# Shifted-window attention on one core: attention outputs computed feature-major in four column groups, softmax weights normalised before their transposition

## What is computed

```python
qkv = xw @ qkvw + qkvb                       # 512 windows of 7x7 = 49 tokens, 160 features
q, k, v = heads(q), heads(k), heads(v)       # 5 heads of 32 features
attn = softmax(einsum('whid,whjd->whij', q, k) * 32 ** -0.5 + bias + mask)
out = einsum('whij,whjd->whid', attn, v)     # back to 49 x 160
out = out @ projw + projb
x = x + out; x = x + gelu(ln(x) @ w1 + b1) @ w2 + b2
```

## Time and profile before

| | us |
|---|---|
| median of three runs | 3516.08 |
| profiled execution, its own time | 3515.67 |
| its span, first to last instruction | 3513.9 |
| TensorE matmuls busy | 3297.9 |
| VectorE busy | 2393.0 |
| ScalarE busy | 1878.0 |
| GpSimd busy | 833.1 |

### The profile page before, as it was taken

The page is one execution under the profiler, slowest core; times in us unless marked ns, Lnnn a source line. Parts: engine busy times, 40 slices in busy tenths (PEclk is TensorE's granted clock), DMA queues, the critical chain, the costliest instruction groups (busy, mean ns, idle before and its releaser), DMA issues. The chain is left out here.

```text
span 3513.9 us, 95515 instructions
## 1 busy us (share of the span) xinstructions
PE 3297.9 (94%) x35820; PEld 2960.7 (84%) x35820; DVE 2393.0 (68%) x6968; ACT 1878.0 (53%) x4454; POOL 833.1 (24%) x1625
## 2 busy tenths in 40 slices
PE   7995999999999999999999999999999999999679
PEld 6884888888888888888888888888888888888579
DVE  1114777777777777777777777777777777777322
ACT  1112555555555555555556666666666666666221
POOL 5300222222222222222222222222222222222110
PEclk9997999999999999999999999999999999999789
DMA  5321111111111111111111111111111111111275
GB/s 108 87 73 47 30 35 34 34 34 34 34 33 30 34 34 34 34 34 44 43 31 32 35 35 29 35 23 35 35 35 29 35 23 35 35 35 24 47 137 92
DMA packets 246486, 148.37 MB, mean 42 GB/s; under 512 B 31429, under 2 KB 245880, under 8 KB 246398
## 3 DMA queue, kind: packets, MB, share of 16 engines
q1 hardware_dynamic: 244694, 147.01, 18.7%
q0 software_dynamic: 1728, 0.48, 0.1%
HBM read 96.80 MB, written 52.50 MB: 42 GB/s over the span
## 5 line engine op out<-in xcount | busy, mean ns | idle before, releaser
L1350 PE MATMUL rm<-w,ht 128*112 128x160 f32 x4480 | 693.7, 304 | 0.0
L1350 PEld LDWEIGHTS rm<-w,ht 128*112 128x112 f32 x4480 | 608.8, 177 | 28.6 <-ACT ht L951 13.0
L951 ACT ACTIVATE ht<-rm 128x448 f32<-128x448 f32 (+1 forms) x640 | 319.2, 499 | 263.5 <-PE rm L111 258.1
L865 POOL TENSOR_TENSOR rs<-ln_tmp,mhalf 112x4 f32<-112x4 f32 (+1 forms) x128 | 125.6, 981 | 996.0 <-DVE ln_tmp L1031 996.0
L933 ACT ACTIVATE ot_hi<-ra 128x98 fp32r<-128x98 f32 x512 | 103.1, 257 | 455.0 <-PE ra L1329 455.0
L896 ACT ACTIVATE qm<-ra,qmask 128x392 f32<-128x392 f32 x512 | 259.0, 589 | 12.1 <-PE ra L111 3.2
L1298 PEld LDWEIGHTS s_ps<-kt,qm 128*49 128x49 f32 x8192 | 210.2, 126 | 48.9 <-issue 40.4
L111 PE MATMUL rm<-z2t_hi,w_hi 128*128 128x448 f32 (+1 forms) x640 | 248.1, 388 | 1.3 <-DVE z2t_rest L1133 1.1
L1298 PE MATMUL s_ps<-kt,qm 128*49 128x49 f32 x8192 | 242.3, 212 | 3.1 <-DVE sc L1091 3.1
L1040 DVE TENSOR_SCALAR z<-xa,mean,rs 112x160 f32<-112x160 f32 x448 | 128.1, 358 | 135.7 <-POOL rs L839 135.7
L1075 DVE TENSOR_SCALAR vb<-ra,kmask 98x320 f32<-98x320 f32 x384 | 205.3, 549 | 20.8 <-ACT vb L915 10.4
(11 more groups left out here) (216 smaller groups left out, 9455.0 us busy)
## 6 DMA issues: line engine op xcount, KB each, us to landing
xa<-xs SPq DMA_DIRECT2D x128, 245.0 KB
xr<-xs SPq DMA_DIRECT2D x128, 245.0 KB
xs<-a_tok SPq DMA_DIRECT2D x8, 1960.0 KB, 9.5
xs<-xo SPq DMA_DIRECT2D x64, 245.0 KB
ys<-yz SPq DMA_DIRECT2D x64, 245.0 KB
c_y<-ys SPq DMA_DIRECT2D x48, 260.0 KB
c_y<-ys SPq DMA_DIRECT2D x16, 280.0 KB
c_taps<-in_f_syn SPq DMA_DIRECT2D x24, 126.0 KB, 4.7
```

The costliest lines, as they stand in the source:

```text
L951: act_(ht[:, f * SN + t0 * TT:f * SN + (t0 + nt) * TT], bank_m(i, lm, use)[:, 0:nt * TT], ACT.Gelu_apprx_tanh).then_inc(m_freed(i, lm, use ...
L1350: last = mm(bank_m(i, lm, use)[0:TT, t * DIM:(t + 1) * DIM], ht[:, c:c + TT], keep.w["w2", lm][:, f * DIM:(f + 1) * DIM], start=(f == 0), ...
```

## The change

The outputs are computed with features on partitions. For this the values are the stationary operand (32 columns, one head) and the transposed weights the moving one (49 columns). Heads 0 to 3 go to partitions 0, 32, 64 and 96 of `o_ps`, head 4 three times to 0, 32 and 64 at column OC = 196, as the split of the last 32 features wants it; 7 x 2 x 2 = 28 products per group. Outputs land in the order of the image rows, and ScalarE and VectorE take them from `o_ps` directly, in two operations each instead of four. The output transposes, `os_` and the four OT uses of the ring are gone. The column of ones is gone; VectorE sums `pr` instead, and GpSimd multiplies `pr` by the reciprocal into `pn` (one buffer) ahead of the transposition. The transposition's second operand is a permuted identity, `gather`, which brings the two windows' queries side by side (49 + 49). The lists of all engines are reordered. In the diff `weights_normal` is GpSimd's, `exps` and `weights_out` are ScalarE's, `weights_summed` is VectorE's (in place of its `outputs`), `weights_turned` and the last `outputs` are TensorE's.

```diff
+                def weights_normal(j):
+                    n = i * NG + j
+                    pool.wait_ge(s_rec, n + 1)
+                    reach(pool, s_ptf, n)
+                    gp.tensor_tensor(pn[:].rearrange("q (g k) -> q g k", k=WT), pr[:].rearrange("q (g k) -> q g k", k=WT),
+                                     view(rd, 0, QP, 0, [[1, 2 * HEADS], [0, WT]]), ALU.mult).then_inc(s_pn, 1)
...
                 def exps(j):
                     act.wait_ge(s_ssub, i * NG + j + 1)
+                    reach(act, s_pn, i * NG + j)
                     act_(pr[:], sm[j % 2][:], ACT.Exp).then_inc(s_exp, 1)
                 def weights_out(j):
-                    act_(pt[:, 0:4 * QP], pt_ps[0:GK, 0:4 * QP], ACT.Copy)
-                    act_(pt[:, 4 * QP:5 * QP], o_ps[0:GK, PT4:PT4 + QP], ACT.Copy).then_inc(s_pte, 1)
+                    act_(pt[:], pt_ps[0:GK, 0:HEADS * GK], ACT.Copy).then_inc(s_pte, 1)
...
+                def weights_summed(j):
+                    n = i * NG + j + 1
+                    dve.wait_ge(s_exp, n)
+                    v.tensor_reduce(den[:], pr[:].rearrange("q (g k) -> q g k", k=WT), AX.X, ALU.add).then_inc(s_den, 1)
+                    dve.wait_ge(s_den, n)
+                    v.reciprocal(rd[:], den[:]).then_inc(s_rec, 1)
...
                 def weights_turned(j):
-                    pe.wait_ge(s_exp, n + 1)
+                    pe.wait_ge(s_pn, n + 1)
                     reach(pe, s_pte, n)
+                    for h in range(HEADS):
+                        last = tr(pt_ps[0:GK, h * GK:h * GK + QP], pn[:, h * GK:(h + 1) * GK], gather[:])
+                def outputs(j):
+                    n = i * NG + j
+                    pe.wait_ge(s_pte, n + 1)
                     reach(pe, s_od, n)
+                    pe.wait_ge(*a_freed(i - 1, f"V{j}"))
+                    for w in range(2):
+                        for p in range(2):
+                            for g in range(HEADS + 2):
+                                h, row, c0 = (g, g * HD, 0) if g < 4 else (4, (g - 4) * REST, OC)
+                                last = mm(view(o_ps, row, HD, c0 + p * 2 * WT + w * WIN, [[2 * WIN, WIN], [1, WIN]]),
+                                          view(vb, 0, GK, j * VG + ((p * 2 + w) * HEADS + h) * HD, [[1, HD]]),
+                                          pt[:, h * GK + w * WT:h * GK + (w + 1) * WT], start=True, stop=True)
...
-        RA = Ring(["OT0", "OT1", "T1A0", "T1C0", "T1A1", "T1C1", "OT2", "Q0", "K0", "OT3", "P0", "P1", "B0", "Q1", "P2",
-                   "K1", "B1", "V0", "V1", "V2", "V3"], 3, V_READERS)
+        RA = Ring(["T1A0", "T1C0", "T1A1", "T1C1", "Q0", "K0", "P0", "P1", "B0", "Q1", "P2", "K1", "B1", "V0", "V1", "V2",
+                   "V3"], 3, V_READERS)
```

More of the change, by code:

```diff
@@ L924, in weights_out @@
                     act.wait_ge(s_ptf, i * NG + j + 1)
-                    act_(pt[:, 0:4 * QP], pt_ps[0:GK, 0:4 * QP], ACT.Copy)
-                    act_(pt[:, 4 * QP:5 * QP], o_ps[0:GK, PT4:PT4 + QP], ACT.Copy).then_inc(s_pte, 1)
+                    act_(pt[:], pt_ps[0:GK, 0:HEADS * GK], ACT.Copy).then_inc(s_pte, 1)
                 def outputs_hi(j):
[L929 to L934, removed]
+                    act.wait_ge(s_of, i * NG + j + 1)
+                    for dst, rows, c0 in ((ot[0], 128, 0), (ot[2], CR, OC)):
+                        last = act_(view(dst, 0, rows, j * 2 * WIN, [[WIN * W, 2], [W, WIN], [1, 2 * WIN]]),
+                                    view(o_ps, 0, rows, c0, [[2 * WT, 2], [2 * WIN, WIN], [1, 2 * WIN]]), ACT.Copy)
                     last.then_inc(s_oth, 1)
@@ L1047, in _ @@
                 v.memset(t[CR:CK, :].bitcast(F32), 1.0)
[L1048 to L1053, removed]
+            v.tensor_copy(view(gather, 0, QP, 0, [[WT, 2], [1, WT]]), view(keep.ident, 0, QP, 0, [[WP, 2], [1, WT]]))
+            v.tensor_copy(gather[:, GK:QP], keep.ident[0:QP, WT:WP])
+            v.memset(s_ps[:], 0.0).then_inc(s_init, 1)
             def body(i, la, lm, ln):
@@ L1157, in body @@
                 if la is not None:
-                    outputs(0)
-                    scores(2, i, la)
+                    weights_summed(1)
                 if lm is not None:
@@ L1162, in body @@
                 if la is not None:
-                    outputs_lo(0)
-                    outputs(1)
-                    scores(3, i, la)
+                    scores(2, i, la)
                 if lm is not None:
@@ L1388, in body @@
                 if la is not None:
-                    outputs_turned(1)
-                    weights_turned(2)
+                    outputs(0)
+                    scores(3, i)
+                    weights_turned(1)
+                if lm is not None:
+                    mlp_out(3)
+                if la is not None:
+                    outputs(1)
                 if ln is not None:
@@ L1393, in body @@
                 if la is not None:
-                    outputs(2)
+                    weights_turned(2)
                 if ln is not None:
```

126 lines of the change are left out of this document (47 added, 79 removed).

## The result

The changed kernel takes **3614.14 us** (median of four runs, 3608.28 to 3617.03), against 3519.22 us for the kernel before in the same set of runs: ratio **1.0271**, interval 1.0248 to 1.0294. The profiled execution took 3608.28 us, its span is 3606.8 us.

A forecast was written before the change was run, and what follows sets the result against it. TensorE, busy 94% of the span, was taken to bound the kernel; new waits from the lengthened chain add 1.15 us in each of 62 iterations, 71 us: 3515.7 + 71 = 3586 us, range 3530 to 3645.

The forecast's parts named there:

- The wait at T1C1: Transposes of the next front's last part: TensorE waits 2.1 us for VectorE's low half to free their bank.
- TensorE's arrival: TensorE reaches the bank for the next front's last transposes at 13.8 us, while VectorE frees it at 15.9.
- The walk: Step-by-step timing of one phase B iteration across engines; projection begins at 23.8 us against 22.6, possibly wrong by 0.4.
- The second wait: At the projection: TensorE's own work is done at 23.0 us and it waits 0.8 for the last outputs.
- GpSimd's product: New 113x490 weight normalisation on GpSimd, taken as 1.1 us; the next group's exponentials wait for it.
- The products: 28 output products of 49 columns per group, four column groups side by side: 0.77 us without edges.
- the first rival: Two at a time: the 28 products overlap only in twos or are issue-limited, 1.33 us; 3621 us, chance 0.20.
- TensorE's work: Per iteration: -1.56 for transposes, +0.76 for products, +0.4 for layout passages; -0.4 us, or -25 us in all.
- The passages: TensorE going into and out of column groups: seven excursions per iteration instead of six, plus one four-to-two passage, +0.4 us.
- The period: Phase B iteration grows by 1.15 us, from 44.7 to 45.8, in 62 iterations: 71 us.
- The clock: Forecast keeps TensorE's clock at 1.00; separate case: waits bring 1.2 GHz for a time, +73 us, 3659, chance 0.04.
- faster case: VectorE frees the next front's bank before 13.8 us, no wait arises, TensorE's work decides: 3472 us, chance 0.10.

The follow-up runs named there:

- e3: The changed kernel with two buffers instead of one for the exponentials, their sums and the reciprocals; 3515.01 us, ratio 0.9996.
- e8: e4 with the 28 products of a group issued column group by column group instead of going round the groups; 3606.04 us, ratio 1.0259.
- e9: The changed kernel with 9 extra small matmuls (98 rows, 22 columns) in TensorE's wait at T1C1; 3555.18 us, ratio 1.0103.
- e10: The changed kernel with two extra matmuls of 490 columns in TensorE's wait at T1C1; 3560.19 us, ratio 1.0122.
- e4: The changed kernel with two buffers for exponentials, sums and reciprocals, and mlp_out(4) moved ahead of front_turned(1) on TensorE; 3446.13 us, ratio 0.9805.
- e11: e4 with ScalarE's outputs_hi(3) moved ahead of keys(0); 3418.04 us, ratio 0.9714.
- e2: The changed kernel with TensorE's mlp_out(4) moved ahead of front_turned(1), into the wait at T1C1; 3477.30 us, ratio 0.9892.
- e7: The changed kernel with 18 extra small matmuls (98 rows, 22 columns) in TensorE's wait at T1C1; 3712.08 us, ratio 1.0555.

## Why the prediction was right and where it missed

The forecast was the likeliest case and it came: slower, 3614 in a range of 3530 to 3645. By its steps:

- **The wait at T1C1**, predicted 2.1 us: 1.84. TensorE's arrival, predicted 13.8 after the MLP's first output product: 13.74 (1035.39 + 0.45 - 1022.10). That this is so near is luck: by TensorE's blocks from 1022.10 to 1035.84 the scores and products were taken 0.63 us too long with their edges, the MLP pieces and transposes 0.56 too short. The low half of the front, predicted to end at 15.9: it begins at 14.90 and its 0.62 takes it to 15.52. The walk was 0.4 us long there. The second wait, predicted 0.8: 0.61 in the first block, none at the projection in the second.
- **GpSimd's product**, 1.1 taken: 1.01. That the exponentials wait for it is in the row at 1026.80, but once an iteration and not for every group, and e3 prices it: 0.72 us of wait per iteration in the first block, 0.58 in the second.
- **The products**, 0.77 without edges: four groups do work side by side, and the first rival is refuted. The mechanism held as well: a column group takes its products one after another, 0.087 us each (e8) where the forecast had 0.095, and the fullest group's eight make 8 x 0.087 = 0.70 us, the block without its edges. By the rule of the Trainium skill, TensorE: Matmul & The Clock Gate, section Back-to-back issue gap, 56 records would have taken 1.4 us at 25 ns; the trace has 0.83 with all edges, 15 ns a record, with starts 7 ns apart in different groups; in one and the same group they are 43 ns apart (e8). The measurement decides against the rule for this use of the array.
- **TensorE's work**, predicted -0.4 us per iteration: **-1.18**. This step failed. A block of products costs 0.83 with its edges where the kernel before had 0.71, +0.12 four times, not +0.76 and another +0.4 for the passages; less the 1.56 of transposes that is -1.08. The passages priced at 0.4 don't show. The sum and the walk of the prediction did not agree with each other: the walk's own blocks are 13.8 to T1C1 and 7.1 behind it, 20.9 us, where the earlier trace rows has 22.6 less the wait of 0.30; that is 1.4 less, and the separate sum said 0.4 less. The time was taken from the walk, which is why it came out near; no rival or chance but the faster one used the -0.4.
- **The period**, predicted +1.15 us: +0.71 where the clock stays, so -27 us on the forecast.
- **The clock.** This is the term of the sum that was mis-sized, by far. The forecast had it at 1.00 and a separate case, with a chance of 0.04, priced at 73 us. It was 0.98 over phase B and cost 52 to 59 us, in addition to the waits. The size that the case gave it was not far off: a twentieth of phase B at half clock, where 116 us are a twenty-fifth. The mechanism stood there ("waits of 2.1 us in every iteration bring TensorE down to 1.2 GHz for a time"); what failed was to argue from waits of 0.30 us that did no harm to waits seven times as long, and to give that 0.04 while the forecast itself contained the waits.

3516 + 44 + 52 = 3612: the two misses, -27 and +52, and 3 us between the two medians of the kernel before (3516 and 3519), make the 28 between 3586 and 3614. The forecast doesn't owe its place in the range to the clock: without it the kernel takes 3555 to 3560 us (e9, e10), in the range and slower too.

"Slower" was right as the kernel was written, and yet the change is a gain of its own: its work on TensorE is 1.1 us an iteration less, and e4 and e11 show it. The prediction's faster case (3472) named the right condition, VectorE freeing the bank before TensorE comes. It held that the chain would have to be 2.1 us shorter for that, and looked only at the product's length, not at the order of the queues: e2 gets there by moving one block of TensorE's own work, the chain untouched.

## What to carry to other kernels

When a step is moved into a chain that was hidden, ask whose queue it makes late, and then what of TensorE's own work can be put before that wait: one block moved ahead of the waiting transposes was worth more here (137 us) than a second buffer (99 us), which took away 0.72 of the 1.84 us only. A wait of TensorE can have a second price, the clock, that is not in the wait's own length; here waits of 1.8 us had it in every second iteration, at 1.5 us a time, and waits of 1.1 to 1.3 us had not: look at the granted clock by iteration, not over the span, and price it in the forecast as soon as the forecast has such a wait. Products for different column groups must also be issued in turn (0.83 us a block against 1.69).

## What the runs showed of the hardware that was not expected

- The half clock comes after waits of 1.83 to 1.92 us in 33 iterations of 62, after waits of 2.21 us in all 62, after 1.49 us in 7, and after 1.12 us (1.27 in the second block) in none. The length of the wait alone doesn't decide it: in the changed kernel the waits of 1.84 and 1.86 us at 1037.68 and 1083.07 are alike, and only the second is followed by half clock. In that kernel it comes in every second iteration, and four times in two iterations running. What tells one iteration from the next was not tested.
- One stretch of the changed kernel, in iteration 63, follows two shorter waits close together (PEclk is 0.50 from 3360.20 to 3363.60):

```profile
3357.72 0.90 PE L1321 MATMUL o_ps<-pt,vb 98*32 98x49 f32 x56 [0.86 <-ACT pt L942]
...
3360.09 1.46 PE L1321 MATMUL o_ps<-pt,vb 98*32 98x49 f32 x56 [0.85 <-ACT pt L942]
```

- It comes without any idle time too: 3.1 us of matmuls of 22 columns brought it (e7), 1.6 us of the same did not (e9), nor did two of 490 columns (e10). What decides between these was not tried further.
- Products of 98x32 by 49 columns took 0.030 us each when issued round four column groups and 0.060 us each when issued group by group. A column group has a pace of its own, one record in 0.043 us (e8), near the 0.0475 of the scores, and the fullest group sets the length of the block. One after another in one group the 28 products would take 28 x 0.087 = 2.4 us (an estimate from e8's records), so the 0.83 measured is 2.9 times faster; eight of 28 in the fullest group allow 3.5. The Trainium skill, TensorEngine Tiling (Array Packing), section Theoretical Speedup, has up to 4x for 32 columns, which these numbers keep to.
